# Three chunked stages of a graph network kernel: general turns first, chunk ends written out and interleaved, bias terms on GpSimd

## What is computed

```python
def _gru_cell(x, h, wih, whh, bih, bhh):          # GGNN, after each of two steps
    i_r, i_z, i_n = jnp.split(x @ wih.T + bih, 3, axis=-1)
    h_r, h_z, h_n = jnp.split(h @ whh.T + bhh, 3, axis=-1)
    r = jax.nn.sigmoid(i_r + h_r)
    z = jax.nn.sigmoid(i_z + h_z)
    n = jnp.tanh(i_n + r * h_n)
    return (1.0 - z) * n + z * h                  # then relu; after step 2: @ out_w.T + out_b, x + ., layernorm

aggregated = aggregated / jnp.maximum(degree, 1.0)[:, None]      # MPNN
upd_in = jnp.concatenate([node_state, aggregated, g_nodes], axis=-1)
delta = _linear(jax.nn.relu(_linear(upd_in, Wu1, bu1)), Wu2, bu2)
h = node_state + delta                            # then layernorm with ln_g, ln_b; x + ., layernorm
```

## Time and profile before

| | us |
|---|---|
| median of 3 runs | 10035.09 (10032.35 to 10036.63) |
| profiled execution | 10033.66 |
| its span | 10031.9 |
| first GGNN stage (`ggnn0_edges`) | about 4624 to 4923 |
| second GGNN stage | about 6548 to 6932 |
| MPNN stage, the last of the program | about 9719 to 10032 |

### The profile page before, as it was taken

How to read it: one execution, slowest core, us unless ns; L and a number is a source line. 1 busy time by engine, 2 the same in 40 slices (tenths; PEclk the granted TensorE clock), 3 DMA queues, 4 the chain that set the end, 5 groups by cost and what they waited for, 6 DMA issues and landing times. The chain is left out here.

```text
span 10031.9 us, 275228 instructions
## 1 busy us (share of the span) xinstructions
PE 8345.2 (83%) x104317; PEld 6699.0 (67%) x104318; DVE 7403.1 (74%) x11896; ACT 3377.0 (34%) x7132; POOL 2329.2 (23%) x3048
## 2 busy tenths in 40 slices
PE   5777772599959999996699999955886999599983
PEld 4545551599946666664466666635886999499982
DVE  7888888888857666664466766635997888788875
ACT  4777771100015444443244444411330000133321
POOL 2111110000014555553155555510331000100010
PEclk8999995799969999998799999976557999699986
DMA  3333331566633333331233333302772222166650
GB/s 97 110 110 110 110 110 43 164 248 248 248 137 132 115 122 118 121 116 60 68 119 119 121 115 122 114 30 80 302 294 88 94 93 92 66 247 248 248 190 11
DMA packets 393197, 1349.67 MB, mean 135 GB/s; under 512 B 111251, under 2 KB 174781, under 8 KB 354621
## 3 DMA queue, kind: packets, MB, share of 16 engines
q1 hardware_dynamic: 261629, 1054.90, 29.5%
q10 hardware_dynamic: 72704, 173.74, 4.6%
q0 software_dynamic: 58688, 118.70, 3.8%
HBM read 940.84 MB, written 406.28 MB: 134 GB/s over the span
## 5 line engine op out<-in xcount | busy, mean ns | idle before, releaser
L2077 PE MATMUL typed_GP<-typed_hd,typed_Gb 128*128 128x256 bf16 x15288 | 1942.5, 274 | 0.0
L2012 ACT CAST typed_Gb<-typed_GP 128x768 bf16<-128x768 f32 (+1 forms) x1568 | 1336.5, 852 | 1276.0 <-PE typed_GP L2058 635.6
L2077 PEld LDWEIGHTS typed_GP<-typed_hd,typed_Gb 128*128 128x128 bf16 x15288 | 1366.9, 98 | 555.2 <-issue 250.9
L1919 POOL DMA_INDIRECT es_d<-X x1568 | 1574.9, 1004 | 525.1 <-issue 476.7
L1964 DVE TENSOR_TENSOR typed_hd<-typed_recv,typed_iota2b 128x768 bf16<-128x768 bf16 (+1 forms) x1568 | 929.6, 593 | 642.2 <-PE typed_GP L2077 642.0
L1974 DVE CAST typed_Gb<-typed_GP 128x384 bf16<-128x384 f32 (+1 forms) x1568 | 925.1, 590 | 322.5 <-PE typed_GP L2062 166.5
L2058 PE MATMUL typed_GP<-typed_H,typed_hsT 128*32 128x384 bf16 x18816 | 1054.8, 330 | 66.7 <-ACT typed_H L2005 66.7
L719 ACT ACTIVATE prep_OJF<-prep_OJ,prep_fld 128x98 bf16<-128x98 bf16 x3136 | 861.9, 368 | 123.3 <-DVE prep_OJ L783 123.1
L2058 PEld LDWEIGHTS typed_GP<-typed_H,typed_hsT 128*32 128x32 bf16 x18816 | 357.6, 95 | 523.6 <-issue 237.9
L949 PE MATMUL prep_PS<-prep_OJF,prep_OHr 128*128 128x490 bf16 x1582 | 466.7, 461 | 234.2 <-DVE prep_OHr L814 234.2
L1806 PE MATMUL mpnn_GP<-mpnn_hd,mpnn_et 128*128 128x128 f32 x4802 | 578.7, 277 | 2.4 <-issue 1.4
(11 more groups left out here) (576 smaller groups left out, 13893.1 us busy)
## 6 DMA issues: line engine op xcount, KB each, us to landing
typed_rows<-slott_d SPq DMA_DIRECT2D x196, 832.0 KB, 4.2
HB<-slot_d SPq DMA_DIRECT2D x98, 1568.0 KB
es_d<-gcn_blank ACTq DMA_DIRECT2D x49, 3136.0 KB, 10.1
ba_rows<-slot_d SPq DMA_DIRECT2D x49, 3136.0 KB
mpnn_et<-es_d SPq DMA_DIRECT2D x147, 768.0 KB, 4.2
X<-et_d SPq DMA_DIRECT2D x98, 1024.0 KB
heads_rows<-slot_d SPq DMA_DIRECT2D x49, 1568.0 KB
et_d<-wt_early SPq DMA_DIRECT2D x112, 512.0 KB, 2.6
```

The source lines that it names most:

```text
L1919: pool.indirect_dma_start(es_d, bass.IndirectOffsetOnAxis(ap=SI[:, at:at + 1], axis=0), ET[:, i % 2, c, :], None).then_inc(scattered[i % 2 ...
L2012: act.copy(Gb[:, par, 0:2, 0:w], GP[:, 3 * par:3 * par + 2, 0:w]).then_inc(evA, 1)
L2077: mm = pe.matmul(agg(a), gathered(par, ch, k), hd[:, par, ch, :], start=q0 == 0 and ch == 0 and k == 0, stop=False, skip_group_check=True)
```

## The change

- The three stages run all general turns in one loop at the start and then the seven chunk ends, written out with static addresses; `turns` goes away.
- GGNN: two sets of gate buffers (the second lies in `G`, the gathered rows, free after the turns). Products are split into r, z and n with semaphores of their own. Chunk c's products stand ahead of chunk c-1's transposes or out product, and in the second stage chunk c-2's transposes and head products stand behind these. The new state goes to `HB` directly. In the first stage one copy of seven tiles and one DMA from SP replace seven copies and seven DMAs from ScalarE; in the second the norm writes `X` directly.
- MPNN: products read `acc` and `X` in place of ScalarE's copies; chunk c's front (hidden layer) stands ahead of chunk c-1's late part on VectorE. GpSimd makes three terms per chunk with four operations, into two sets of buffers: `has`*bias+bias, `X`+bias U2, `X`+bias LNB. VectorE's five operations of the front before the relu become three; its late part's five tensor operations (norms aside) become three.
- `norm` is split in two (`norm_begin` up to the variance, `norm_finish` from the root on) with the same operations.

The core of the diff (twelve leading spaces cut; lines taken out are described above where not shown):

```diff
     OHf = OH[:].rearrange("p a c n -> p (a c n)")
     buf = [OHf[:, k * CW:(k + 1) * CW] for k in range(4)]
+    if not rest:
+        Gf = G[:].rearrange("p s c f -> p (s c f)")
+        buf += [Gf[:, k * CW:(k + 1) * CW] for k in range(4)]
...
-                with act.Fori(0, NCH) as c:
+                n = act.value_load(to[0:1, NCH:NCH + 1], min_val=1, max_val=KCAP // sl)
+                with act.Fori(0, n) as i:
                     if attr:
-                        turns(act, to, c, items)
+                        items(i)
                     if typed is not None:
-                        turns(act, to, c, sums_of_types)
-                    run.scalar(act, c)
+                        sums_of_types(i)
+                run.scalar_all(act)
...
+            run.pool(pool)
...
-                with dve.Fori(0, NCH) as c:
-                    turns(dve, to, c, items)
-                    t1 = dve.value_load(to[0:1, ds(c + 1, 1)], min_val=0, max_val=KCAP // sl)
-                    dve.wait_ge(added, t1 * sl + sl)
-                    dve.sem_inc(acc_ready, 1)
-                    run.vector(dve, c)
-                    dve.wait_ge(done, c + 1)
+                n = dve.value_load(to[0:1, NCH:NCH + 1], min_val=1, max_val=KCAP // sl)
+                with dve.Fori(0, n) as i:
+                    items(i)
+                dve.wait_ge(added, n * sl + sl)
+                passed(dve, tick)
+                dve.sem_inc(acc_ready, 1)
+                run.vector_all(dve)
...
-                with pe.Fori(0, NCH) as c:
-                    turns(pe, to, c, items)
-                    pe.wait_ge(acc_ready, c + 1)
-                    run.tensor(pe, c)
-                    pe.wait_ge(done, c + 1)
+                n = pe.value_load(to[0:1, NCH:NCH + 1], min_val=1, max_val=KCAP // sl)
+                with pe.Fori(0, n) as i:
+                    items(i)
+                pe.wait_ge(acc_ready, 1)
+                run.tensor_all(pe)
...
+sets = [[halves(b) for b in buf[4 * k:4 * k + 3]] for k in range(2)]
...
+    def products(self, pe, c, free):
+        x_ = [acc[:, c * CW + a * HW_:c * CW + (a + 1) * HW_] for a in range(2)]
+        h_ = [HB[:, c * CW + a * HW_:c * CW + (a + 1) * HW_] for a in range(2)]
+        for k, (read, prod) in enumerate(((sig_r, rprod), (sig_z, zprod))):
+            if c:
+                pe.wait_ge(read, c)
+            free(k)
+            for a in range(2):
+                pe.matmul(gp[k][:, a, :], W(W_IH + 3 * l + k), x_[a], start=True, stop=False)
+                mm = pe.matmul(gp[k][:, a, :], W(W_HH + 3 * l + k), h_[a], start=False, stop=True)
+            mm.then_inc(prod, 1)
+        if c:
+            pe.wait_ge(pre, c)
+        free(2)
         for a in range(2):
+            pe.matmul(gp[2][:, a, :], W(W_IH + 3 * l + 2), x_[a], start=True, stop=True)
+            mm = pe.matmul(gp[3][:, a, :], W(W_HH + 3 * l + 2), h_[a], start=True, stop=True)
+        mm.then_inc(nprod, 1)
...
+    def gates(self, act, c):
+        rg, zg, ng = sets[c % 2]
         rz = C_RZ + 3 * l
+        act.wait_ge(rprod, c + 1)
+        if c >= 2:
+            act.wait_ge(hready, c - 1)
+        act.activation(rg, gp[0], ACT.Sigmoid, bias=bcol[:, rz:rz + 1]).then_inc(sig_r, 1)
+        act.wait_ge(zprod, c + 1)
+        act.activation(zg, gp[1], ACT.Sigmoid, bias=bcol[:, rz + 1:rz + 2]).then_inc(sig_z, 1)
+    def squash(self, act, c):
+        ng = sets[c % 2][2]
         act.wait_ge(pre, c + 1)
         act.activation(ng, ng, ACT.Tanh, bias=bcol[:, C_IH + 3 * l + 2:C_IH + 3 * l + 3]).then_inc(tanhed, 1)
 
...
+        dve.wait_ge(sig_z, c + 1)
...
-        V.tensor_scalar(hs, rg, 0.0, None, ALU.max).then_inc(hready, 1)
+        V.tensor_scalar(h_, rg, 0.0, None, ALU.max).then_inc(hready, 1)
...
+    def tensor_all(self, pe):
+        def z_free(c, k):
+            if k == 1 and c >= 2:
+                pe.wait_ge(tcopied, c - 1)
+        for c in range(NCH + 1):
+            if c < NCH:
+                gru.products(pe, c, lambda k: z_free(c, k))
+            if c:
+                m = c - 1
+                pe.wait_ge(gru.ready, m + 1)
+                pe.wait_ge(gru.z_read, min(c + 1, NCH))
+                if m:
+                    pe.wait_ge(tcopied, m)
+                turn_tiles(pe, tp, HB[:, m * CW:(m + 1) * CW]).then_inc(tprod, 1)
...
+    def sync(self, sp):
+        for m in range(NCH):
+            sp.wait_ge(tcopied, m + 1)
+            sp.dma_start(h_d[1][m * CW:(m + 1) * CW].rearrange("(t p) f -> p t f", p=P),
+                         tiles3(tb[:, m % 2])).then_inc(stored[m % 2], 16)
...
+        def banks_free(c, k):
+            if k == 0 and c >= 2:
+                pe.wait_ge(lifted, c - 1)
+            if k == 1 and c >= 3:
+                pe.wait_ge(xcopied, c - 2)
+            if k == 2 and c >= 3:
+                pe.wait_ge(kept, c - 2)
+        for c in range(NCH + 2):
+            if c < NCH:
+                gru.products(pe, c, lambda k: banks_free(c, k))
+            read = min(c + 1, NCH)
+            if 1 <= c <= NCH:
+                m = c - 1
+                pe.wait_ge(gru.ready, m + 1)
+                pe.wait_ge(gru.r_read, read)
+                if m:
+                    pe.wait_ge(lifted, m)
+                times(pe, op_, HB[:, m * CW:(m + 1) * CW], W(W_OUT)).then_inc(oprod, 1)
+            if c >= 2:
+                m = c - 2
+                pe.wait_ge(normed, m + 1)
+                pe.wait_ge(gru.z_read, read)
+                if m:
+                    pe.wait_ge(xcopied, m)
+                turn_tiles(pe, tp, X[:, m * CW:(m + 1) * CW]).then_inc(xturned, 1)
+                pe.wait_ge(xcopied, m + 1)
+                pe.wait_ge(gru.n_read, read)
+                if m:
+                    pe.wait_ge(kept, m)
+                times(pe, xp, xT, wall[:])
+                times(pe, sp_, xT, wa[:], width=2 * H).then_inc(heads, 1)
...
+    def vector_all(self, dve):
+        own, late = gru.chain(dve), Chain(dve, nchain)
+        for c in range(NCH + 2):
+            if c < NCH:
+                gru.begin(dve, own, c)
+            if 1 <= c <= NCH:
+                m = c - 1
+                r, r3 = buf[4 * (m % 2) + 3], tiles3(buf[4 * (m % 2) + 3])
+                dve.wait_ge(oprod, m + 1)
+                dve.wait_ge(x_back, 16)
+                V.tensor_tensor(out=r, in0=X[:, m * CW:(m + 1) * CW], in1=op_, op=ALU.add).then_inc(lifted, 1)
+                dve.wait_ge(lifted, m + 1)
+                late.step(V.tensor_tensor(out=r3, in0=r3, in1=rows(bias[:, B_OUT, :], TC), op=ALU.add))
+                norm_begin(late, r, st, var_ready)
+            if c < NCH:
+                gru.end(dve, own, c)
+            if 1 <= c <= NCH:
+                norm_finish(dve, late, r, st, rooted, m + 1, X[:, m * CW:(m + 1) * CW]).then_inc(normed, 1)
+            if c >= 2:
+                m = c - 2
+                dve.wait_ge(heads, m + 1)
+                late.step(V.tensor_copy(S[:, m * TC:(m + 1) * TC, :], sp_.rearrange("p (t s) -> p t s", t=TC)))
+                V.tensor_copy(HB[:, m * CW:(m + 1) * CW], xp).then_inc(kept, 1)
+        dve.wait_ge(kept, NCH)
...
+    def pool(self, pool):
+        own = Chain(pool, pchain)
+        for c in range(NCH):
+            w, x2, xl = (lift[:, c % 2, k] for k in range(3))
+            if c >= 2:
+                pool.wait_ge(done, c - 1)
+            own.step(nc.gpsimd.tensor_tensor(out=tiles3(w), in0=over(has[:, c * TC:(c + 1) * TC], D),
+                                             in1=rows(bias[:, B_V, :], TC), op=ALU.mult))
+            own.step(nc.gpsimd.tensor_tensor(out=tiles3(w), in0=tiles3(w), in1=rows(bias[:, B_U1, :], TC), op=ALU.add))
+            own.step(nc.gpsimd.tensor_tensor(out=tiles3(x2), in0=tiles3(chunk(X, c)), in1=rows(bias[:, B_U2, :], TC), op=ALU.add))
+            nc.gpsimd.tensor_tensor(out=tiles3(xl), in0=tiles3(chunk(X, c)), in1=rows(bias[:, B_LNB, :], TC),
+                                    op=ALU.add).then_inc(lifts, 1)
...
+        take_x(0)
+        for c in range(NCH + 1):
+            if c:
+                act.wait_ge(uturned, c)
+                if c >= 2:
+                    act.wait_ge(delta, c - 1)
+                act.copy(uT, tu).then_inc(ucopied, 1)
+                root(act, st, var_ready, rooted, c - 1, 2, 0)
+            if c + 1 < NCH:
+                take_x(c + 1)
+            if c:
+                root(act, st, var_ready, rooted, c - 1, 2, 1)
...
+    def vector_all(self, dve):
+        own = Chain(dve, nchain)
+        r3 = tiles3(r)
+        for c in range(NCH + 1):
+            if c < NCH:
+                u, u3, att = us[c % 2], tiles3(us[c % 2]), slice(c * TC, (c + 1) * TC)
+                dve.wait_ge(uprod, c + 1)
+                if c >= 2:
+                    dve.wait_ge(uturned, c - 1)
+                V.tensor_tensor(out=u3, in0=tiles3(mp), in1=over(cntinv[:, att], D), op=ALU.mult).then_inc(mread, 1)
+                dve.wait_ge(mread, c + 1)
```

(68 more changed lines are left out.)

194 lines of the change are left out of this document (78 added, 116 removed).

## The result

The changed kernel took 9655.31 us, the median of four runs (9647.68 to 9660.65), beside 10035.36 for the kernel before: a ratio of 0.9621, 95% interval 0.9604 to 0.9638. The forecast was 9672. In the profiled execution the span fell from 10031.9 to 9651.7, by 380.2 us.

A forecast was written before the change was run, and what follows sets the result against it. The three stages were taken as bound by a chain from engine to engine, not by work or transfers. Savings of 118 (GGNN 1), 155 (GGNN 2) and 89 (MPNN), 362 us off 10033.7, gave 9672; range 9636 to 9728.

The forecast's parts named there:

- Bare gathers and turn, GGNN: Start of both GGNN stages: products wait for the first 14 gathers, about 16 us bare, then a 65.8 us turn.
- GGNN cycles: Chunk-end periods: 10.8 us in GGNN 1, TensorE the bound; about 17.9 in GGNN 2, TensorE and VectorE within 0.5.
- The drain there: End of GGNN 2: last gates, lift, normalise, transposes, copies and head products after the last chunk's products, 31.7 us.
- rival B: GGNN cycles: pauses lower TensorE's clock; 1.8 us in each of 12 cycles gives 9693, 1.2 GHz throughout 9801; 15%.
- Half clock in chunk 0: First gate products after the GGNN turn: 3.5 us at half clock, costing 1.8 us more, 10.8 in all.
- MPNN, the largest miss: MPNN stage: ends start at 9768, cycles take 23.9 us, 175 us in sum to 9943, 89 us saved.
- GpSimd's operations: MPNN bias terms: 2.1 us an operation with its gap, 8.7 for four in series; nearest row gives 2.03.
- rival C: MPNN: GpSimd slow on broadcast operands; 4 us an operation adds 38, 9710; at the 1.2 bound 9654; 10%.
- The new wait: MPNN chunks 2 to 6: VectorE idles some 6 to 7 us before the front's third operation, released by GpSimd.
- Contention: MPNN: GpSimd beside VectorE's two operations with one side in PSUM costs nil; otherwise 2.2 us in 5 chunks, 11 us.
- Rival D: All 21 written-out chunk ends: engines pause for new code at each, the gain goes, 10055 us or more; 2%.
- Rival E: All three stages: the overlap doesn't come about because misread waits make each stage serial, about 10000 us; 2%.

The follow-up runs named there:

- the split: Changed kernel with three signals in place of one for GpSimd's four operations per MPNN chunk, the first two waiting only for `hidden`: 9639.55 us.
- the terms left out: Changed kernel without GpSimd's four bias operations in the MPNN ends or the wait for them; VectorE's adds read X instead: 9626.50 us.
- The filler: Changed kernel with 14 small matmuls, results never read, in TensorE's pause for ScalarE's copy in each GGNN 2 chunk: 9660.53 us.
- the serial run: Changed kernel with each chunk's first gate product waiting for the end of the previous chunk's gates, in both GGNN ends: 9746.72 us.

## Why the prediction was right, step by step

The total missed by 17 us (0.17%), and no term had the wrong sign.

*Bare gathers and turn, GGNN.* In GGNN 1 products were forecast 92.1 us after the stage's first copy and measured 92.1 (4720.27 less 4628.16). That this is exact is luck: two terms missed by 2.5 us and cancelled. The gathers kept TensorE idle until 28.8 after the copy, not 26.3, and the turn took 63.3, not 65.8 (its first 56 records 8.04 where the earlier trace rows has 9.03). In GGNN 2 it was 27.9 and 63.6. The mechanism, turn first and gathers bare, came as forecast.

*GGNN cycles.* Forecast 10.8 and 17.9, measured 10.64 and 17.45. In GGNN 2 the sum of the four came out (71.7 forecast, 72.4 measured) because the three shorter ones and the one of 20.03 balance. The drain there was put some 2.3 us too high (31.7, measured 29.4). The bounds were named rightly: in GGNN 1 TensorE with a wait for the copied bank (0.62 us), in GGNN 2 TensorE with VectorE's `kept` 0.50 behind. TensorE's pause for the copy in GGNN 2 was 1.98 us, not the 1.1 of rival B, since the transposes before it took 0.93 at full clock and not 1.8.

*Half clock in chunk 0.* None was paid: after a 1.53 us pause the products ran at 1.00, where 2.13 had been followed by 0.52. That gave some 1.7 us back in each stage, in GGNN 1 by luck. The repeat of the changed kernel had the same pause, and its first products came at half clock; timeline and windows (TensorE, its weight loads and the others as in the earlier trace rows) of that run:

```profile
4721.42 1.07 PE L2302 MATMUL ggnn_edges_PS<-acc,wt_early 128*128 128x448 f32 x2 [1.52 <-DVEq L1488]
4722.28 1.70 PE L2303 MATMUL ggnn_edges_PS<-HB,wt_early 128*128 128x448 f32 x2
```

```profile
4721.42:4725.42 4.00, 4.00 (x7) 1.99 (x8) 0.00 (x0) 0.00 (x0) 0.00 (x0) 0.60 0.00 0
```

It was so in 8 of the 11 profiles with these ends (0.60 to 0.65 over the first 4 us; from first product to first gate operation 11.11 in place of 9.41), and in none of the 11 in GGNN 2. So the 1.8 of the forecast was right in size (1.70), and the length of the pause doesn't decide alone. What does stays open.

*MPNN, the largest miss (13.5 us).* The step that failed is the size of four terms, each a little high; the path through a cycle was right. Start: the ends began 46.0 after the stage's first copy, not 49; 2.0 of that came from the gathers themselves, the last of which started 39.7 after the copy and not 41.7, 1.2 from the estimate of 5 us behind them. Fill: 30.7 from the first transposes to the first `done`, not 34.5, and by another path than the sum's. The sum had TensorE's work for chunk 1, priced at half clock (8.5), between the first VectorE operation and the transposes of the hidden layer. It took 4.7 (9492.53 to 9497.27), and what those transposes waited for was chunk 0's front on VectorE, 6.9 long with 2.9 us of contention that the sum didn't have. Cycle: 22.69, not 23.9, from GpSimd's 8.2 in place of 8.7 and a late part of 12.75 in place of 13.4. End: 0.7.

*GpSimd's operations.* Source view of the changed kernel, ns least/median/most:

```profile
L2609 POOL TENSOR_TENSOR mpnn_edges_lift<-has,bias x7: 1682/1685/1705, 9481.9 to 9608.8; 128x896 f32<-128x896 f32 x7
...
L2611 POOL TENSOR_TENSOR mpnn_edges_lift<-mpnn_edges_lift,bias x7: 2068/2069/2090, 9483.7 to 9610.5; 128x896 f32<-128x896 f32 x7
```

1.69 with both operands broadcast and 2.07 with one: the 2.03 from the widest row was near, and rival C falls.

*The new wait.* Forecast were some 6 to 7 us of idle on VectorE before the third operation of fronts 2 to 6 and none in 0 and 1; measured 6.06 in each of the five and none in the others. That it was the wait which set the chunk is shown by the split and the terms left out.

*Contention.* Taken as nil for the front's first two operations, rightly: they took 1.09 beside GpSimd. It was missed elsewhere: in chunk 0 the third and fourth took 2.20 and 2.38, 2.9 us more. The rule of the Trainium skill named in the prediction ("SBUF — State Buffer", on who interferes with whom) fits every row here: the additions with one operand in PSUM (1.09) and bn_stats (1.45) weren't held up, those with two SBUF inputs and the relu were. The same page says the loser of the shared port is blocked for the other's whole instruction and doesn't get a share, and the ends in the split kernel agree to 0.15 us.

*Rival B* came about in small: one GGNN 2 cycle of four paid 2.6 us, not each 1.8. The filler shows the pause as its cause in the cycles. In the eight profiles with these cycles and no filler there was one such cycle each, in three of them a second of 18.34, and in one (one set of gates) the interval of 14.48; in the two with a filler there was none of these. *Rival D*: no idle time of TensorE's matmuls, VectorE or ScalarE at a new chunk is put down to issue, and 21 ends at 10.6 to 22.7 us leave no room for it. *Rival E* falls with the serial run: the overlap is worth 87 us.

## What to carry over

When work is moved to an idle engine, look at when its buffer comes free: two buffers freed by the last reader of a chunk give no lead, and the helper lands on the path; a signal for each reader took the wait away without memory. Then place the helper's operations beside those it doesn't hold up, since a wait removed can return as contention (3.2 of 6.06 us here). In an overlapped chain on TensorE, count what a pause does to the clock as well as its length; and if you fill pauses, size the filler for the shortest one that it will stand in. Before a small difference is put down to an edit, compare the granted clock of the same stretch: the 1.7 us of the run with one set of gates were the clock's.
